# One more gathered column of a pair moved from indirect DMAs to one-hot matmuls in a graph layer

## The reference

```python
def _L0_gnn_ref(x, edge_index, edge_attr, W1, b1, W2, b2):
    rol, col = (edge_index[0], edge_index[1])
    e_feat = jnp.concatenate([x[rol], x[col], edge_attr], axis=-1)
    h = jax.nn.relu(e_feat @ W1 + b1)
    v = h @ W2 + b2
    x_cand = jax.ops.segment_max(v, col, num_segments=num_nodes)
    return jnp.maximum(x_cand, x[:, -v.shape[-1]:])
edge_index = jnp.stack([src, dst])
h = jnp.maximum(_layernorm(x, axis=-1), 0.0)
x = x + _L0_gnn_ref(h, edge_index, edge_attr_32, L0_gnn_W1, ...)
```

## Time and profile before

| | |
|---|---|
| median of 3 runs | 4758.86 us (4730.09 to 4797.8) |
| profiled execution | 4765.93 us, of which the span of its instructions is 4764.1 us |
| mean granted TensorE clock | 0.801 |
| busy share of the span | PE 62%, PEld 44%, DVE 44%, ACT 16%, POOL 57% |

### The profile page before, as it was taken

The page is one execution under the profiler, slowest core; times in us unless marked ns, Lnnn a source line. Parts: engine busy times, 40 slices in busy tenths (PEclk is TensorE's granted clock), DMA queues, the critical chain, the costliest instruction groups (busy, mean ns, idle before and its releaser), DMA issues.

```text
span 4764.1 us, 41821 instructions
## 1 busy us (share of the span) xinstructions
PE 2960.5 (62%) x11492; PEld 2111.3 (44%) x11492; DVE 2078.8 (44%) x3562; ACT 748.1 (16%) x1058; POOL 2733.4 (57%) x2852
## 2 busy tenths in 40 slices
PE   1266566567676666666666666565766656565677
PEld 0144344445454444444444444444544444444445
DVE  5044344444444444444444444343444434444447
ACT  3011111111111111111111111111111111111111
POOL 6456555556665556565566556555655555565550
PEclk8578778788787878887888887778878888787788
DMA  4322222222222222222222222222222222221222
GB/s 99 76 58 53 46 54 47 52 49 59 49 53 47 56 50 55 50 54 47 53 51 51 54 49 51 51 47 52 55 48 50 47 53 51 49 58 43 53 52 44
DMA packets 245595, 252.33 MB, mean 53 GB/s; under 512 B 83265, under 2 KB 199479, under 8 KB 239113
## 3 DMA queue, kind: packets, MB, share of 16 engines
q10 hardware_dynamic: 20790, 103.55, 9.1%
q1 hardware_dynamic: 133938, 101.54, 7.4%
q0 software_dynamic: 90784, 46.48, 7.1%
HBM read 239.86 MB, written 11.52 MB: 53 GB/s over the span
## 4 chain that ended last, share of the span: by engine, by line
another core or an unknown queue 44%; PE 21%; DVE 15%; issue 14%; DVEq 3%; ACT 3%; ACTq 1%; SPq 0%; DMA 0%; POOL 0%; POOLq 0%
PE ps_spare L570 11%; DVE sel_tmp L958 3%; DVE running L929 3%; DVE best L995 3%; PE ps_turned L603 2%; DVE key_hot L947 2%; DVEq L989 2%; PE ps_hid L582 2%; PE ps_val L591 1%; PE ps_feat L537 1%; PE ps_hid L580 1%; DVE edge_hot L940 1%; PE ps_picked L612 1%; DVE feat L965 1%
## 5 line engine op out<-in xcount | busy, mean ns | idle before, releaser
L480 POOL DMA_INDIRECT feat<-h_rows,idx x2821 | 2716.6, 963 | 1900.3 <-issue 993.3
L570 PE MATMUL ps_spare<-table,key_hot 128*128 128x448 f32 x5642 | 1500.6, 426 | 395.6 <-DVE sel_tmp L958 348.0
L570 PEld LDWEIGHTS ps_spare<-table,key_hot 128*128 128x128 f32 x5642 | 1259.8, 230 | 524.3 <-DVE sel_tmp L958 339.0
L958 DVE SCALAR_TENSOR_TENSOR sel_tmp<-off_place,offset,ps_spare 128x448 f32<-128x448 f32 x403 | 273.6, 679 | 1553.4 <-remote 1234.1
L603 PE MATMUL ps_turned<-ident,running 128*128 128x128 f32 x806 | 171.9, 351 | 939.4 <-DVE running L929 733.7
L722 ACT ACTIVATE hidden<-ps_hid,b_col 128x1024 f32<-128x1024 f32 x202 | 224.8, 1113 | 2681.5 <-remote 2196.6
L603 PEld LDWEIGHTS ps_turned<-ident,running 128*128 128x128 f32 x806 | 116.2, 175 | 1088.5 <-DVE running L929 805.1
L980 DVE TENSOR_TENSOR ends<-ps_turned,ends 128x512 fp32r<-128x512 f32 x202 | 139.5, 690 | 786.4 <-ACT ends L734 579.8
L995 DVE TENSOR_TENSOR best<-ps_picked,best 32x64 f32 x1612 | 355.0, 220 | 162.9 <-remote 96.6
L947 DVE TENSOR_TENSOR key_hot<-dst_rows,ps_iota 128x1792 fp32r<-128x1792 f32 x202 | 406.1, 2011 | 18.1 <-DMA dst_rows<-key_rows 18.1
L580 PE MATMUL ps_hid<-feat_t,w_blk 128*128 128x512 f32 x806 | 413.8, 595 | 0.0
(11 more groups left out here) (125 smaller groups left out, 893.7 us busy)
## 6 DMA issues: line engine op xcount, KB each, us to landing
dst_rows<-loc_rows ACTq DMA_DIRECT2D x98, 512.0 KB
feat_t<-attr_rows_in ACTq DMA_DIRECT2D x98, 512.0 KB
feat<-h_rows,idx POOLq DMA_INDIRECT x2821
dst_rows<-key_rows SPq DMA_DIRECT2D x101, 256.0 KB
term_ring<-term_rows SPq DMA_DIRECT2D x404, 64.0 KB
dst_rows<-keep_rows SPq DMA_DIRECT2D x100, 256.0 KB
term_rows<-best SPq DMA_DIRECT2D x3, 1792.0 KB
idx<-src_cols_in SPq DMA_DIRECT2D x51, 32.0 KB
```

Source lines behind the costliest of these rows:

```text
L480: nc.gpsimd.indirect_dma_start(feat[:, slot, k, :], None, h_dram, bass.IndirectOffsetOnAxis(ap=idx[:, c % IDX, k:k + 1].bitcast(U32), axis=0),
L570: mm = pe.matmul(ps_sel, key_hot[:, c // TWO % 2, g, P * (c % TWO):P * (c % TWO) + P], table[half][:, g, :], start=(g == 0 and half == 0), ...
L958: nc.vector.scalar_tensor_tensor(out=sel_tmp[:].rearrange("p (f a) -> p f a", a=SA), in0=off_place[:].unsqueeze(1).broadcast_to([P, D, SA] ...
```

## The change

Three of a pair's sixteen columns are now selected by TensorE and thirteen gathered: the even chunk gathers seven columns, the odd one six. Selections are counted by columns j (three a pair: one of the even chunk, two of the odd), and each has its own one-hot (`key_hot` has 4 of them, made one column at a time, four columns ahead, right behind `take_selected`). `select(j)` writes the PSUM bank j % 2, so it no longer waits for the column just before it, but for the one before that. To free a bank, the result of `pick_ends` shares the bank `ps_turned` with that of `turn_ends`; `turn_ends` gets a wait for `best_taken`, which `keep_best` posts. `key_ring` becomes a tensor of its own, `term_ring` moves to its place, and the tensors that the head needs for the keys lie in `x_even`, with the waits that this takes in the head.

```diff
+SEL = 3
+HOTS = 4
...
+        def gathered(c):
+
+            return COLS - 1 - c % TWO
+
+        def is_column(i, j):
+
+            return not known(i) or j < SEL * (NP - 1) + 1
+
+        def column(j):
+
+            n = j % SEL
+            return TWO * (j // SEL) + min(n, 1), COLS - 1 - n // 2
...
@@ GpSimd
-                for k in range(GK):
+                for k in range(gathered(c)):
                     nc.gpsimd.indirect_dma_start(
...
@@ TensorE
-                pe.wait_ge(S["sel_ready"], i * UNROLL + TWO * v + n)
+                pe.wait_ge(S["sel_ready"], i * (SEL * UP) + (SEL * v + (SEL if n > 1 else 1)))
...
-            def select(i, c):
-                pe.wait_ge(S["hots_made"], i * UP + c // TWO + 1)
-                if not known(i) or c > 0:
-                    pe.wait_ge(S["sel_step"], i * UNROLL + c)
+            def select(i, j):
+                pe.wait_ge(S["hots_made"], i * (SEL * UP) + j + 1)
+                if not known(i) or j > 1:
+                    pe.wait_ge(S["sel_step"], i * (SEL * UP) + j - 1)
                 for g in range(SG):
                     for half in range(2):
-                        mm = pe.matmul(ps_sel, key_hot[:, c // TWO % 2, g, P * (c % TWO):P * (c % TWO) + P],
-                                       table[half][:, g, :], start=(g == 0 and half == 0),
-                                       stop=(g == SG - 1 and half == 1))
+                        mm = pe.matmul(ps_sel[j % 2], key_hot[:, j % HOTS, g, :], table[half][:, g, :],
+                                       start=(g == 0 and half == 0), stop=(g == SG - 1 and half == 1))
...
             def turn_ends(i, v):
-                if not later(i, v):
+                if later(i, v):
+                    pe.wait_ge(S["best_taken"], i * UP + v)
+                else:
                     pe.wait_ge(S["check_step"], 7)
...
             def step(i, v):
+                ahead = [j for j in range(SEL * v + SEL, SEL * v + 2 * SEL) if is_column(i, j)]
...
                 turn_features(i, v)
-                if is_chunk(i, TWO * v + 2):
-                    select(i, TWO * v + 2)
+                for j in ahead[0:1]:
+                    select(i, j)
                 if later(i, v):
                     second_layer(i, v - 1)
+                for j in ahead[1:2]:
+                    select(i, j)
                 if later(i, v - 1):
                     pick_ends(i, v - 2)
-                if is_chunk(i, TWO * v + 3):
-                    select(i, TWO * v + 3)
+                for j in ahead[2:3]:
+                    select(i, j)
...
@@ VectorE
+            def take_selected(i, j):
+                c, k = column(j)
...
+                if is_column(i, j + HOTS):
+                    place_keys(i, j + HOTS)
...
                 place_edges(i, v)
-                if is_chunk(i, TWO * v + 2):
-                    take_selected(i, TWO * v + 2)
-                if is_chunk(i, TWO * v + 4):
-                    place_keys(i, v + 2)
+                for j in ahead[0:2]:
+                    take_selected(i, j)
                 if later(i, v - 1):
                     keep_best(i, v - 2)
-                if is_chunk(i, TWO * v + 3):
-                    take_selected(i, TWO * v + 3)
+                for j in ahead[2:3]:
+                    take_selected(i, j)
```

More of the change, by code:

```diff
@@ L61, in gnn_layer @@
     assert FULLP < P and T == SA * SG
-    CPAD = sel_rows.shape[0]
+    NSEL = sel_rows.shape[0]
+    NSB = -(-NSEL // P)
     SN = SA * D
@@ L71, in gnn_layer @@
     keep_dram = nc.dram_tensor("keep_rows", (Q, C, 2 * P), BF16, kind="Internal").ap()
-    key_dram = nc.dram_tensor("key_rows", (CPAD, P), F32, kind="Internal").ap()
+    key_dram = nc.dram_tensor("key_rows", (NSEL, P), F32, kind="Internal").ap()
     def rows_of(b):
@@ L162, in gnn_layer @@
         keep_ring = shared[:, LOCS:LOCS + KEEPS].bitcast(BF16).rearrange("p (r n) -> p r n", n=2 * P)
-        key_ring = shared[:, LOCS + KEEPS:LOCS + 2 * KEEPS].bitcast(F32).rearrange("p (r e) -> p r e", e=P)
+        term_ring = shared[:, LOCS + KEEPS:LOCS + 2 * KEEPS].bitcast(F32).rearrange("p (r e) -> p r e", e=P)
+        spare = x_even[:].rearrange("p t d -> p (t d)")
+        key_stage = spare[:, 0:NSB * P].rearrange("p (b e) -> p b e", e=P)
+        key_src = spare[:, NSB * P:2 * NSB * P].bitcast(I32).rearrange("p (b e) -> p b e", e=P)
+        off_src = spare[:, 2 * NSB * P:2 * NSB * P + NSEL].bitcast(I32)
+        off_key = spare[:, 2 * NSB * P + NSEL:2 * NSB * P + 2 * NSEL]
         any_dst = loc_ring[0:1, 0:2, :].rearrange("p r e -> p (r e)").bitcast(I32)
@@ L169, in gnn_layer @@
         ps_turned = pb("ps_turned")
-        ps_picked = pb("ps_picked")
         ps_iota = pb("ps_iota")
-        ps_spare = pb("ps_spare")
+        ps_spare = [pb(f"ps_spare{n}") for n in range(2)]
+        ps_picked = ps_turned
         ps_flag = ps_turned[:, 2 * P:3 * P]
-        ps_sel = ps_spare[:, 0:SN]
-        ps_made = [ps_val, ps_spare]
-        end_bank = [ps_feat[:], ps_hid[:, 0, :], ps_turned[:], ps_picked[:]]
+        ps_sel = [bank[:, 0:SN] for bank in ps_spare]
+        ps_made = [ps_val, ps_spare[0]]
+        end_bank = [ps_feat[:], ps_hid[:, 0, :], ps_hid[:, 1, :], ps_turned[:]]
         ps_place = ps_iota[:, 0:WIN]
@@ L187, in gnn_layer @@
             chunk_begun feat_turned feat_t_ready edge_hot_ready hid_sum hid_ready val_sum val_ready
-            best_half run_ready ends_turned ends_ready ends_split pick_ready best_done best_zero
+            best_half best_taken run_ready ends_turned ends_ready ends_split pick_ready best_done best_zero
             check_step worst_ready flag_turned flag_ready
@@ L367, in _ @@
             sp.wait_ge(S["key_made"], 1)
-            for b in range(-(-CPAD // P)):
-                r = min(P, CPAD - b * P)
+            for b in range(NSB):
+                r = min(P, NSEL - b * P)
                 sp.dma_start(key_dram[b * P:b * P + r, :], key_stage[0:r, b, :]).then_inc(S["key_out"], 16)
@@ L390, in _ @@
             sp.wait_ge(S["h_stored"], EVEN)
+            sp.wait_ge(S["key_out"], 16 * NSB)
+            sp.wait_ge(S["off_step"], 5)
             win_dmas(sp.dma_start, x, x_even, False, 0, T, S["x_win_in"])
@@ L638, in _ @@
             pe.wait_ge(S["table_ready"], 2)
-            for c in range(TWO):
-                select(0, c)
+            for j in range(SEL):
+                select(0, j)
             steps(pe, step, {1: turn_worst})
@@ L997, in keep_best @@
                         mm.then_inc(S["best_half"], 1)
-                if known(i) and v == NP - 1:
-                    mm.then_inc(S["best_done"], 1)
+                mm.then_inc(S["best_done" if known(i) and v == NP - 1 else "best_taken"], 1)
             def step(i, v):
+                ahead = [j for j in range(SEL * v + SEL, SEL * v + 2 * SEL) if is_column(i, j)]
                 if later(i, v - 1):
@@ L1028, in _ @@
             dve.wait_ge(S["firsts_in"], 16)
-            for v in range(2):
-                place_keys(0, v)
-            for c in range(TWO):
-                take_selected(0, c)
+            for j in range(HOTS):
+                place_keys(0, j)
+            for j in range(SEL):
+                take_selected(0, j)
             steps(dve, step, {1: check})
@@ L1096 @@
     given["attr_rows"] = by_feature.reshape(-1, len(begins) * 4 * P)
-    picked = np.stack([np.asarray(src)[a:a + CE].reshape(2, P, Q)[1, :, Q - 1] for a in padded])
+    blocks = [np.asarray(src)[a:a + CE].reshape(2, P, Q)[1] for a in padded[0:len(begins) + len(begins) % 2]]
+    picked = np.stack([block[:, q] for n in range(0, len(blocks), 2)
+                       for block, q in ((blocks[n], Q - 1), (blocks[n + 1], Q - 1), (blocks[n + 1], Q - 2))])
     given["sel_rows"], given["sel_cols"] = picked, picked.T
```

72 lines of the change are left out of this document (33 added, 39 removed).

## The result

The changed kernel takes 5259.53 us (median of 4 runs, 5255.96 to 5264.1), and the kernel before 4756.03 us (4 runs, 4730.09 to 4797.8) in the same comparison: a ratio of 1.105, with the interval 1.097 to 1.113. The profiled execution took 5262.41 us (span 5260.5) at a mean granted clock of 0.836. It is 496.5 us longer than the profiled execution before. The prediction was 5480 us: the sum of its terms, 708 us more than before, is 5467, and it was rounded up a little. Ratios in this document compare fast runs of both kernels alone, so that one can differ a little from the quotient of two medians.

A forecast was written before the change was run, and what follows sets the result against it. It took the bound to be TensorE's posts held until after each gather burst, not a busy engine. +3.5 us a pair by 194 pairs (679), with 24 and 5, added 708 to 4759: 5467, stated as 5480 us, range 4980 to 5800.

The forecast's parts named there:

- The sign: Whole kernel: the change makes it slower, given a chance of 0.82; faster had 0.13.
- The burst: GpSimd's run of gathers for a pair: 13 DMAs take 15.95 us, 1.3 less than 17.3.
- the pair held to the end: Pair whose late TensorE posts wait until after the burst: 29.5 us after the change, 25.6 before; half of all pairs.
- the hold: Among the gathers: what TensorE posts late in a burst is seen by other engines only 3.0 us after it.
- the border: Some 6 us from the burst's start: TensorE posts made earlier are seen at once, later ones held.
- let through, but the third misses: Pair whose early posts pass mid-burst while the third select's waits until behind it: 24.5 us, +3.9; two of three let-through pairs.
- the likeliest case: The chain as forecast, together with the rival of TensorE's time alone: 5250 to 5800 us, chance 0.74.
- half and half: Held and let-through pairs taken as equally frequent, from 78 and 80 waits: mean 23.1 us before, 26.6 after.
- Behind the gathers: The 8 pairs after the last gather: 3.0 us more of busy TensorE each, 24 us in all.
- Mostly let through: Rival: most pairs become the good kind at 22.1 to 24.5 us; 4670 to 5140 us, chance 0.12.
- Faster: Rival: the pause behind the burst stays and each pair loses one gather, 243 us off; 4545 us, chance 0.13.
- Only TensorE's time: Rival: TensorE at a low clock bounds, adding 3.0 to 3.9 us a pair; 5370 to 5540 us, within the 0.74.

The follow-up runs named there:

- f3: The changed kernel with the 14th gather put back, into a spare tile that nobody reads: 5597.25 us, ratio 1.124 to the kernel before.
- h3: The changed kernel with VectorE's scan ahead of the third take, selects one pair further ahead, and the 14th gather kept in a spare tile: 4894.06 us, ratio 1.002.
- f1: The changed kernel itself again, on a chip where the kernel before took 4988.74 us: 5312.36 us, ratio 1.067.
- f2: The kernel before without the last gather of every odd chunk and nothing in its place: 4670.9 us, ratio 0.940.
- g2: The changed kernel itself again, on a chip where the relu begins 0.04 us after its matmul: 3447.03 us, ratio 0.944 to the kernel before.
- e1: The changed kernel with two selected columns instead of three, so 14 gathers a pair: 3644.16 us, ratio 0.998 to the kernel before.
- e4: The changed kernel with one gather for each chunk, leaving out 11 of a pair's 13: 3447.05 us, ratio 0.944 to the kernel before.
- e3: The changed kernel with GpSimd's burst waiting for the first select behind turn_features, some 3 us later: 3446.86 us, ratio 0.944 to the kernel before.
- scan first: The changed kernel with VectorE's scan ahead of the third take and selects one pair further ahead; with 13 gathers 3397.98 and 3399.02 us, both ratio 0.931.

## Why the prediction came out as it did

**The sign held, and the mechanism in outline, on the chips that the forecast was for.** The kernel loses because the third `select` puts a post that the next scan needs too late into the burst, so that the pause behind the burst grows (9.05 us for 5.5). f3 and h3 show it: the same gathers and the same three selects are at 1.124 in one order and at 1.00 in the other (two holding chips), and the pause is nearly the same with 13 and with 14 gathers (9.25 and 9.5 us, f1 and f3).

**The burst** was given as 15.95 us and is 16.15. Its worth of 1.3 us a pair was measured at 1.5 (f3 against f1) and 1.6 us (f2 against the kernel before).

**The term that was mis-sized is the pair held to the end, 29.5 us, and its share of one half.** It put take, one-hot, `keep_best`, take, one-hot and scan behind the hold, since I had set the border at some 6 us into the burst and the second `select` (6.8) and `pick_ends` (7.9) lay beyond it. I had written that I would be wrong if the second `select`'s post is seen at once. It is: made at 7.1 us, taken 0.13 us later in the timeline above. VectorE's own view of the takes among the gathers (idle before, us, times) counts them:

```profile
L981 DVE SCALAR_TENSOR_TENSOR sel_tmp<-off_place,offset,ps_spare x548: 679/681/685, 402.5 to 4995.1; 128x448 f32<-128x448 f32 x183
...
  remote: 901.3, 176
  PE ps_spare L589: 584.6, 228
  issue: 283.3, 138
```

176 waits of 5.1 us end with "remote", one in 183 pairs of three takes each; the other two takes of a pair have short ones. `keep_best` begins inside the burst as well, in 176 of 182 pairs. So hardly a pair is of the 29.5 us kind. Nearly all are of the kind "let through, but the third misses", which the prediction gave 24.5 us; the period above is 24.85, and the mean 25.2. Had I taken that kind for every pair, the sum would have been 194 x (24.5 - 23.1) = 272, with 24 and 5 some 5060 us, by the measured 22.7 for before 5137. The other 120 us are, in the main, the 0.7 us by which the pair is longer than 24.5. The measured time lies 10 us above the bottom of the likeliest case's own range (5250 to 5800), so that it falls into this range is in part luck. The step that failed is thus the one that carried the half and half of the kernel before over to the changed one. Why the early posts pass in nearly every pair now no run isolates.

The half and half was itself misread. It took the counts 78 and 80 of the earlier trace rows for the two kinds, but these go by the releaser's name; by length a third of the pauses (63 of 178) were long. With a third the working gives 22.3 us before, nearer to the measured 22.7, and 25.6 after. That is +3.4 a pair for its +3.5, so this slip alone moved the sum little.

**A part of the pair is TensorE's clock.** On the open chip the changed kernel's transposes take 0.63 (L623), and the first `select` behind them 3.08 us; in the pair above 1.09 and, for the `select` at its burst's start, 4.18 (3.6 to 5.1 over the trace). The granted clock is 0.84 in the window among the gathers here, and 1.00 in the like window of g2. TensorE stands idle for 7.8 us ahead of L623 on the holding chip and for 0.8 us on the open one. The prediction's 2.76 us for transposes and restart had this in it, taken from the rows before.

**Behind the gathers** a pair takes 16.0 us and not 15.2, for VectorE's chain leaves TensorE the gap of 0.8 us seen in g2: 8 x (16.0 - 12.2) = 30 us for the 24 given. With 481 for the pairs that makes 511, so -15 us are left for the head and for what the means leave out, where I had +5 and a bound of -10.

**The two banks, the shared bank and the key loads** were costed at nothing, and e1 agrees on an open chip.

**The rivals.** "Mostly let through" (4670 to 5140) had the better picture of the early posts, but its price (22.1 to 24.5) needed the third to be caught in many pairs, and it never is: in all full bursts of the trace the third take begins behind the burst. "Faster", 4545 us, is wrong on the holding chips and right on the open ones, where there is no hold: 0.944 (g2), since a gather less takes the pace from 17.6 us a pair to the 16 of TensorE and VectorE. So even the sign of the forecast needed a result measured where the profile before was, on an occasion with a hold: on four of the seven occasions it would have been wrong. The rule behind it, in the Trainium skill, "SBUF — State Buffer", section "Who interferes with whom", is that DMA never contends with a compute engine. On open chips the rows agree (e4: 11 gathers fewer change nothing). On holding chips they don't look so: the relu begins 4.15 us after its matmul in the pair above and 0.04 us after it on an open chip. But e4 never ran on a holding chip, so that the gathers cause the hold there rests on its timing (in the changed kernel all 182 relus begin 2.3 to 3.0 us behind a burst's last gather). No single trace of a holding chip could have told me of the other kind. "Only TensorE's time" fails by its rows: TensorE stands idle 7.8 us a pair.

**What stays open.** What holds the posts and TensorE, and why it is there on some occasions and not on others, no run here shows. Nor is the border a plain time since the burst began: `pick_ends` passes at 8.0 us in the changed kernel (2725.43, `keep_best` at 2727.39) and is held at 6.6 us in h3. e1's form, e3's later burst and e4's single gathers never ran on a holding chip, nor did scan first with 13 gathers. By h3's 1.002 and the 5 to 6% that a gather is worth there (f1 against f3, f2), my estimate for the last is 0.94 to 0.95 on a holding chip; 0.931 is measured on two open ones. It is the version that I would take: faster than both kernels where it ran, and by the estimate on the other chips too.

## What to carry to other kernels

When one engine's wait has the releaser "remote" in a one-core kernel, compare the time at which the releasing instruction ended with the time at which the waiter began, and order the consumer's work so that nothing urgent stands behind the late post: moving one scan ahead of one take, with the selects one pair further ahead, was worth 11% here, as much as the added matmuls had cost. Before trusting a model of such a wait, run the unchanged kernel on a second chip, since the same change was 10.5% slower on one and 5.6% faster on another. When a mix of two kinds of period is carried over to a changed kernel, work out which posts decide between them and price the pure cases first, since the mix is itself a result of the timing that is changed.

## What the runs showed of the hardware

The kernel before was timed on seven occasions (six chips of the record, and the result's, whose number it doesn't give), and they fell into two kinds: 3651 to 3653 us on four, 4756 to 4989 us on three. On the three, posts of TensorE that are made late in a run of indirect DMAs reach ScalarE and VectorE only 2.4 to 3.6 us after the last of these has ended (2733.54 to 2735.89 in the changed kernel, 2725.73 to 2729.31 in h3), up to 14.9 us after the matmul (2715.04 to 2729.89 in h3). The posts of VectorE that the record has are not late in these bursts (2725.30 in the changed kernel, 0.01 us after its end), and TensorE can stop along with its posts (2.7 us in the median in h3). On the four, the relu begins 0.04 us after its matmul (g2). I had not expected chips of one type to differ in this. An indirect gather of 128 rows costs GpSimd 0.94 us and 0.30 us behind it on both kinds, so a kernel that issues them without pause is bound by 1.25 us for each.
